# A burst of matmuls moved between two pairs of score matmuls in an attention and mixture-of-experts kernel

## What is computed

```python
x = L0_attn_x                                    # 4 x 512 x 256, float32
xn = _layernorm(x)
x = x + attention(xn) + moe(xn)

# attention: 8 key/value heads of width 8, 4 query groups, so 32 query heads
q, k, v = xn @ Wq.T, xn @ Wk.T, xn @ Wv.T
scores = einsum('bsqhd,bthd->bqhst', qh, kh) / sqrt(8)
a_dot = einsum('bqhst,bthd->bsqhd', softmax(scores), vh)
a_mem = elu(q) @ memory / (elu(q) @ memory_norm)
out = a_dot * (1 - w) + a_mem * w                # w = sigmoid(memory_weight)

# moe: top 2 of 8 experts with silu gates of width 512, plus a shared expert of width 1024
```

## Time and profile before

| | |
|---|---|
| time, median of 3 runs | 822.18 us (821.41 to 827.67) |
| profiled execution, device time | 823.77 us |
| its span, first to last instruction | 821.9 us |
| mean granted TensorE clock | 0.985 |
| busy: PE, DVE, ACT, POOL | 726.3, 486.6, 423.2, 150.3 us |

### The profile page before, as it was taken

How to read it: one execution, slowest core, us unless ns; L and a number is a source line. 1 busy time by engine, 2 the same in 40 slices (tenths; PEclk the granted TensorE clock), 3 DMA queues, 4 the chain that set the end, 5 groups by cost and what they waited for, 6 DMA issues and landing times.

```text
span 821.9 us, 13441 instructions
## 1 busy us (share of the span) xinstructions
PE 726.3 (88%) x3824; PEld 340.4 (41%) x3825; DVE 486.6 (59%) x675; ACT 423.2 (51%) x803; POOL 150.3 (18%) x265
## 2 busy tenths in 40 slices
PE   5999999877878878878878787899999999998997
PEld 2455445211111111111111111466666666667887
DVE  5275688777888888888888880112222221214854
ACT  2463401577788888888888777322222222224422
POOL 1000002655532222121222121000000000003740
PEclk9999999699999999999999999999999999999999
DMA  9537100357210111100111252051111111111431
GB/s 318 209 110 274 30 0 15 117 167 228 82 52 20 30 30 30 30 24 22 30 30 30 83 193 83 14 205 39 51 43 46 45 45 48 42 39 58 118 101 52
DMA packets 51278, 65.35 MB, mean 80 GB/s; under 512 B 9496, under 2 KB 44208, under 8 KB 51248
## 3 DMA queue, kind: packets, MB, share of 16 engines
q1 hardware_dynamic: 40192, 40.85, 15.7%
q10 hardware_dynamic: 7984, 15.73, 5.7%
q0 software_dynamic: 3072, 8.39, 3.2%
HBM read 40.15 MB, written 24.38 MB: 79 GB/s over the span
## 4 chain that ended last, share of the span: by engine, by line
PE 80%; ACT 9%; issue 3%; POOL 3%; DMA 2%; DVE 1%; SPq 1%; ACTq 0%; DVEq 0%; POOLq 0%
PE ps L1294 16%; PE ps L1276 14%; PE ps L1309 11%; ACT att L689 8%; PE ps L1353 8%; PE ps L1154 7%; PE ps L1385 5%; PE ps L1181 4%; PE ps L1146 3%; PE ps L1400 3%; PE ps L1344 2%; PE ps L1114 2%; PE ps L1265 1%; PE ps L1111 1%; POOL acc L526 1%
## 5 line engine op out<-in xcount | busy, mean ns | idle before, releaser
L938 DVE TENSOR_REDUCE smax<-ps 128x2 f32<-128x1024 f32 x256 | 304.2, 1223 | 57.1 <-PE ps L1181 56.3
L689 ACT ACTIVATE att<-ps 128x512 f32<-128x512 f32 x512 | 277.3, 597 | 86.4 <-PE ps L1309 81.7
L1309 PE MATMUL ps<-att 51*128 51x512 bf16 x512 | 101.9, 394 | 72.8 <-ACT att L689 70.5
L1294 PE MATMUL ps<-big,xn 128*128 x312 | 140.9, 594 | 1.9 <-ACT oT_sb L662 1.3
L1276 PE MATMUL ps<-att,v_head 128*32 128x512 f32 x1024 | 140.7, 622 | 0.1
L1018 DVE COPY xn<-ps 128x512 f32<-128x512 f32 x39 | 27.0, 691 | 170.1 <-PE ps L1344 170.1
L1309 PEld LDWEIGHTS ps<-att 51*128 51x128 bf16 x512 | 25.5, 93 | 244.0 <-ACT att L689 215.3
L1181 PE MATMUL ps<-att 48*128 48x512 bf16 x512 | 100.4, 387 | 1.4 <-DVE smax L938 1.4
L1294 PEld LDWEIGHTS ps<-big,xn 128*128 128x128 f32 x312 | 58.9, 190 | 61.5 <-issue 59.7
L564 POOL DMA_INDIRECT xn<-slot_y,slot x32 | 33.6, 1052 | 237.2 <-DMA slot_y<-xn 227.8
L1353 PE MATMUL ps<-big,xn 128*128 x312 | 73.7, 380 | 0.1
(11 more groups left out here) (149 smaller groups left out, 648.9 us busy)
## 6 DMA issues: line engine op xcount, KB each, us to landing
big<-w ACTq DMA_DIRECT2D x8, 1024.0 KB
q_stacks<-big SPq DMA_DIRECT2D x12, 512.0 KB
att<-q_stacks SPq DMA_DIRECT2D x64, 96.0 KB, 2.1
slot_x<-zeros SPq DMA_DIRECT2D x1, 4992.0 KB, 17.2
e_x<-slot_x SPq DMA_DIRECT2D x39, 128.0 KB, 2.0
slot_y<-xn SPq DMA_DIRECT2D x39, 128.0 KB, 1.7
big<-w ACTq DMA_DIRECT2D x8, 512.0 KB
att<-k_stacks SPq DMA_DIRECT2D x64, 48.0 KB, 2.1
```

The lines of the kernel that those rows point to most:

```text
L689: act.activation(probs[:, t % 2, g, :], ps[:, RING[turn_of(u) % 3], :], ACT.Exp, scale=SCALE)\
L938: dve.reduce_max(smax[:, s % 2, :].rearrange("p (half v) -> p half v", half=2)[:, :, v], ps[:, bank:bank + 2, :], X_AXIS).then_inc(max_don ...
L1294: last = pe.matmul(ps[:, 4 * a + n, :], e_xT[:, a, k, :], w, start=k == 0, stop=k == KD - 1)
L1309: pe.matmul(ps[:, RING[turn_of(2 * v + half) % 3], :], k_st[s][rows, P * t:P * (t + 1)], q_st[s][rows, g, :], start=True, stop=True).then_ ...
```

## The change

TensorE's order within a quarter changes. Before, the burst of weighted values stood behind both score pairs with their maxima matmuls, and behind the transpositions. Now it stands behind the first score pair and its maxima matmuls, ahead of the second score pair. The waits inside `weighted_values` move with it. Nothing else differs, and the other engines' programs are the same.

```diff
                         if ahead:
                             scores_for_max(i + 2, (s + 2) % 4, blk + (s + 2) // 4, v)
+                        if g == 0:
+                            if t > 0:
+                                weighted_values(i, s, t - 1, pair)
+                            elif not first:
+                                weighted_values(i - 1, s + 3, ST - 1)
                     if t == MAX_AT // G - 1 and not last:
                         transpose_max(i + 1, s + 1)
                     if t == OUT_AT // G - 1 and s % 2 == 0 and not first:
                         transpose_o(pair - 1, (s // 2 + 1) % 2)
-
-                    if t > 0:
-                        weighted_values(i, s, t - 1, pair)
-                    elif not first:
-                        weighted_values(i - 1, s + 3, ST - 1)
```

## The result

The changed kernel takes 848.01 us (median of 3 runs, 847.7 to 856.5) against 822.18: a ratio of 1.0329, 95% interval 1.0255 to 1.0403. It is slower, as forecast, and 10 us under the 858 of the forecast, 1 us above the lower end of its own range (847). The profiled execution has a span of 845.8 us, 23.9 over that of before, at a mean clock of 0.984 (before 0.985).

The account below looks back on a forecast made before the run. A loop of waits between score matmuls and exponentials was taken to bound the attention. To 822.2 us it added 32 for waits (33.3 - 1.1 + 0.6 - 0.8) and 4 for the clock: 858, own range 847 to 866.

Parts of the forecast that it names:

- The bound: Attention: score matmuls and exponentials wait for each other in a loop; no engine is full. Score matmuls sat idle 72.8 us.
- An ordinary quarter: Idle time moves from ahead of the second score pair to ahead of the next quarter's first; 2.69 against 2.71, cost 0.
- The ring's turns: Quarters 0 and 2: skipped turns of three banks make the next score pair wait one exponential more, 0.52 us each.
- The copy: Quarter 1 of every even head but the first: the burst waits for ScalarE's accumulator copy, 1.02 us over an ordinary quarter.
- The sum of a pair: Odd head +0.88 and even head +1.34 make a pair of heads 24.62 us against 22.40, +2.22.
- S0 to its first exponential 0.50: Time from a quarter's first score pair to its first exponential, 0.50 us; also used behind the second pair.
- The early heads: Heads 0 and 1, quarter 2 of head 0: +0.6; two early heads ending in waits for maxima rows grow less: -0.8.
- The last head: Quarters 1 and 2, ending in expert matmuls, fall from 4.42 and 4.40 to 3.75 and 3.55; whole head -1.1.
- The clock: Idle stretches in even heads bring three or four short falls to half clock, +4 us; 0 to 7 falls, 0 to +8.
- Falls in most even heads: Rival: eight to fifteen falls lasting over a quarter, +10 to +75 on 854, most likely 868 to 890; chance 0.27.
- The ring for less: Rival: skipped bank turns cost less than 0.52 each, only the 1.02 in 15 even heads is paid: 838; chance 0.10.
- Faster, by the filled idle time: Rival: idle 0.55 ahead of the second score pair is filled, nothing else becomes late: 750, half of it 785; chance 0.05.

Follow-up runs that it names:

- after_split: Changed kernel, but TensorE waits for each score unit's bank right ahead of that unit's matmul, not for both banks ahead of the pair: 836.95 us, ratio 1.0257.
- all_but_q1even: Changed kernel, but in quarter 1 of even heads the burst stands behind both score pairs as before: 832.44 us, 1.0128 against the kernel before.
- q1only: Kernel before, with the burst moved between the score pairs in quarter 1 alone: 844.42 us, 1.0255 against the kernel before.
- after_no_pvwait: Changed kernel without ScalarE's wait, ahead of a quarter's first exponential, for the burst two quarters back: 851.80 us, 1.0355 against the kernel before.
- copy_early: Changed kernel with ScalarE's accumulator copy moved from quarter 1 to ahead of the third exponential of quarter 0: 832.42 us, 1.0127 against the kernel before.
- m_between: Kernel before with both pairs of maxima matmuls ahead of the second score pair, burst still behind it: 815.90 us, ratio 0.9921.
- before_no_pvwait: Kernel before without ScalarE's wait, ahead of a quarter's first exponential, for the burst two quarters back: 821.17 us, ratio 1.0011.
- m_between_rows: Kernel before with both maxima matmuls ahead of the second score pair, and each third of the maxima rows sent when made: 807.51 us, ratio 0.9872.

## Why the prediction was right

- **The bound.** A loop between exponentials and scores, not an engine: right. after_split shows by which unit it closes.
- **An ordinary quarter costs nothing.** Right in kind. Forecast 2.69, measured 2.61 (quarter 3 at 302.81, quarter 1 of odd heads). The idle time moved from S1 to the next S0.
- **The ring's turns.** Forecast 0.52 in quarters 0 and 2 of every head, measured 0.49 (3.10 against 2.61), without the copy's price in all_but_q1even. The 0.52 was the mean over four exponentials of which the third had to wait for its scores; two that follow each other start 0.49 apart.
- **The copy.** Forecast 1.02, measured 1.02 in q1only.
- **The sum of a pair.** Forecast +2.22, measured +1.46. All eight quarters are 0.08 to 0.11 shorter than forecast, 0.76 together. Some 0.12 of that is the ring's 0.03 in four quarters. The rest is the term that was mis-sized most, "S0 to its first exponential 0.50": 0.42 behind S1 in the new order (301.25 to 301.67 and the like), since the second wait of ScalarE is not on that exponential. It was carried over from S0, where it was measured. Of a row I knew that it could be 0.43 and put it in the bounds only. Over 15 pairs the 0.76 are 11 us; the forecast was 10 too high.
- **Luck in the total.** The waits alone were forecast at +32 with bounds of +25 to +36. They measured some 22, below the bounds, because a pair came out at 23.86 and the bounds allowed for 0.5 under 24.62. The medians differ by 25.8, which is 2 more than the profiled pair and some 4 more than the waits, and so 848.01 lies just inside the range from 847. The mechanism was right; that the total fell within the range was in part luck.
- **The early heads.** Forecast +0.6 and -0.8. These can't be told apart from the clock, which fell elsewhere in the two executions (heads 0 to 5 took 75.4 us before and 73.2 after).
- **The last head.** Forecast -1.1, measured +0.05 (503.96 to 518.39 before, 526.13 to 540.61 after). The quarter with the first expert matmuls was forecast at 3.75 and took 4.66 (529.18 to 533.84), the next one 3.89 for 3.55. The first expert matmuls I took to follow right behind S1. They wait for ScalarE's copy of their operand, which it makes behind the seventh exponential:

```profile
530.50 0.39 PE L1309 MATMUL ps<-att 51*128 51x512 bf16 x2
...
531.93 1.55 PE L1294 MATMUL ps<-big,xn 128*128 x3 [1.04 <-ACT xn L669]
```

- **The clock.** Forecast three or four short falls in even heads at +4. There were three, where forecast: the bursts at 175.66, 489.75 and 516.40, which had waited 1.03, 1.03 and 1.25 us for the copy, stand just ahead of them. The twelve others had waited 0.95, and none of them was followed by a fall. The first two falls cost about 2.5 us each (15.0 for a head of 12.44), twice my price. The expected net of +4 didn't show in the profiled pair, because before had lost as much. Over the runs: kernels with the copy's 1.0 wait had clocks of 0.967 to 0.986 (changed, q1only, after_no_pvwait), those without 0.981 to 0.994 (all_but_q1even, copy_early), which fits the reasoning without proving it: the profiled run of all_but_q1even fell too, without that wait, and the kernel before had runs at 0.979.
- **The rivals.** Falls in most even heads: not seen; none in heads 5 to 26. The ring for less: ruled out by all_but_q1even, where a turn costs 0.49. Faster, by the filled idle time: the point that I named decides, the exponential behind S1 comes too late. m_between and its followers show the filling that does work.

## What to carry to other kernels

Idle time on an engine that works in order is worth filling only with work that the loop doesn't then wait behind. The burst took 1.00 us where 0.55 was free, pushed the next score pair back and won nothing even in an ordinary quarter, while 0.22 us of matmuls fitted. Before moving a group of instructions, list the waits that it carries (here one for ScalarE's copy) and what will be queued behind them. Where buffers are taken in turns, write down for each user which earlier one it waits for: a skipped turn makes it wait for a later one. Once a loop gets shorter, chains that had slack end last next (here the maxima rows, VectorE and the ring's turns), so edits that do nothing alone may be worth something together.

## What the runs showed of the hardware that was not expected

- A second semaphore wait ahead of an instruction on ScalarE cost 0.07 us although its condition had long been met (0.50 against 0.43 from scores to exponential, in three quarters of four), 0.24 us a head. In quarter 1, which has the same two waits, it was 0.43 with both (281.88 to 282.31 before) and 0.42 with one (309.23 to 309.65 in before_no_pvwait); why is open.
- The time of one and the same kernel moves with the granted clock from run to run: before took 816.07 us at a mean of 0.995 and 824.21 at 0.983. A difference of 5 us could be read in the trace's steady heads to the hundredth of a microsecond, and not in the medians of ten and nineteen runs, though it shows when runs of equal clock are compared.
- Away from the clock's falls, steady heads of one kind repeated to 0.02 us, except for m_between's odd heads (10.60 to 10.69) and one head of m_between_rows (11.44 for 11.38).
